# Selection matrices of a two-part graph network made three or four slots at a time

## The chip, the cores and the metric

One core of a Trainium2 chip runs the whole kernel in one launch. The metric is device time in microseconds (us) of that core. A core has five engines that run side by side and meet at semaphores: TensorE (PE, matrix products), VectorE (DVE), ScalarE (ACT), GpSimd (POOL, which here issues the gathers) and SyncE (SP, which issues transfers).

## The reference, cut to what matters

A graph with 6250 nodes of 128 features and 100,000 edges is passed through two relational layers and then two attention layers. Each layer gathers a row for each edge and sums the rows of the edges that end in the same node.

```python
def _rgcn_layer(h, src, dst, rel, basis, w_comp, loop_w, bias):
    W = jnp.einsum('rb,bio->rio', w_comp, basis)
    seg = dst * N_REL + rel
    agg = jax.ops.segment_sum(h[src], seg, num_segments=N_ENT * N_REL)
    msg = jnp.einsum('nri,rio->no', agg.reshape(N_ENT, N_REL, -1), W)
    return jax.nn.relu(msg + h @ loop_w + bias)

def _gat(x, src, dst, W, a_src, a_dst, b):
    xw = (x @ W).reshape(n, H, FH)
    e = jax.nn.leaky_relu(al_s[src] + al_d[dst], 0.2)
    ee = jnp.exp(e - jax.ops.segment_max(e, dst, num_segments=n)[dst])
    alpha = ee / jax.ops.segment_sum(ee, dst, num_segments=n)[dst]
    return jax.ops.segment_sum(alpha[:, :, None] * xw[src], dst, num_segments=n) + b
```

## The kernel before, in words

**Slots.** The edges are sorted by their end node and cut into tiles of 128 edges. A slot is one tile with one window of 128 end nodes; there are NS = 832 slots in each of the four layers. The sum of a slot is one matrix product: the gathered rows (128 edges by 128 or 136 columns, in the ring `Gr`) are multiplied by a selection matrix of 128 by 128 (in the ring `Sr`), which holds 1 where the edge's end node, `DL[:, s]` (one number in each partition), equals the column's number, `iota`. VectorE builds that matrix with one comparison, and later adds the product, which lies in a PSUM bank of `B`, to the window's sum in `AC`, a part of `XA`.

**Relational layers.** VectorE's loop runs over the slots: it makes the matrix of slot s + 8 (`selr`, a ring of SRR = 15; line 924 of the profile), waits for the product of slot s - 2 (`slot_mm`) and adds it (L935). TensorE (L1837) waits for the bank to be free (`slot_add`) or, for the first three or four slots, for `built_v`, and then for the tile to have landed, which SP relays. GpSimd's stream is one indirect gather for each tile (L2081), 782 of them in a layer, into a ring of 64 tiles; each reads 128 row numbers from `GID`.

**Attention layers.** The slots are worked on in 26 chunks of 32. While a chunk's 32 products run, the next chunk is prepared by generators that step once for a slot in its first 12 slots, and then once in two. The first eight steps of VectorE's `prep` make four matrices each (`sel`, a ring of 64; L1027). ScalarE waits for all four (`sel_made`) and casts them to bf16 in one copy of 512 columns (L1526), TensorE turns them, and softmax work follows. VectorE also weighs the gathered rows (L1103) and adds the products (L1128), and now and then weighs a finished window (L588). GpSimd gathers 830 tiles in a layer (L2098) by row numbers in `SRC`, into a ring of 96.

All orders are written out in program order on each engine; no scheduler moves anything.

Of the kernel before, what the change touches and what calls it, by code (L numbers as in the profile page):

```python
# [9 lines left out]
P = 128  # L10
# [7 lines left out]
NS = 832  # L18
# [7 lines left out]
SR = 64  # L26
TG = 64
SRR = 15
# [8 lines left out]
BIG = 1.0e30  # L37
EPS = 1e-5
LOOK, LAG = 8, 2
HS = NS // 2  # L40
HW = NW // 2
SLOW_STORES = (24, 30)
# [71 lines left out]
def build(nc, I, out, dbg=None):  # L114
# [3 lines left out]
    ALU = mybir.AluOpType  # L118
# [3 lines left out]
    with ctx:  # L122
# [14 lines left out]
        Sr = sb("Sr", [P, SR * P])  # L137
# [183 lines left out]
        def selr(s):  # L321
            return Sr[:, s % SRR * P:(s % SRR + 1) * P]

        def sel(s):
            return Sr[:, (s % SR) * P:(s % SR + 1) * P]

        def G3(c, a, b):
            o = (c * CH) % GR
# [487 lines left out]
        def vector(e):  # L816
# [85 lines left out]
            for L in range(2):  # L902
                if L == 0:
                    e.wait_ge(params, PARAMS)
                    e.wait_ge(tv.sem, tv.at("rstd"))
                    e.wait_ge(row_v, 3 * NW)
                    e.wait_ge(tg.sem, tg.at("of31"))
                    e.wait_ge(ta.sem, ta.at("oft1"))
                if L == 1:
                    for u in range(NW + NTURN - 3, NW + NTURN):  # L910
                        wait_store(e, u)
                    e.memset(x3[:, NW - 1, :], 0.0).then_inc(x0_clear, 1)
                if L == 0:
                    for u in range(NW - 3, NW):
                        wait_store(e, u)
                turn = iter(())

                def start(k):
                    return onward_vector(e, k, wregs) if L == 0 else outward_vector(e, k, wregs, xregs)
                for s in range(-LOOK, NS + LAG):  # L920
                    sn = s + LOOK
                    if sn < NS:

                        e.tensor_scalar(out=selr(sn), in0=iota[:, :], scalar1=DL[:, sn:sn + 1], scalar2=None,  # L924
                                        op0=ALU.is_equal).then_inc(built_v, 1)
                    sa = s - LAG
                    if sa >= 0:
                        if sa % 16 == 0:
                            e.reg_load(vregs[sa % 32 // 16], OFF[0:1, sa:sa + 16])
                        e.wait_ge(slot_mm, L * NS + sa + 1)  # L930
                        if vpos["self"]:
                            e.wait_ge(row_self, vpos["self"])
                            vpos["self"] = 0
                        a = AC[:, bass.ds(off(e, vregs[sa % 32 // 16][sa % 16], NW * CW), P)]
                        ins = e.tensor_tensor(a, a, B[RGCN_BANKS[L][sa % len(RGCN_BANKS[L])]][:, 0:P], ALU.add)  # L935
                        if L or sa:

                            ins._wait_ge(slot_add, L * NS + sa)
                        ins.then_inc(slot_add, 1)
                        vpos["add"] = L * NS + sa + 1  # L940
                        if L == 0 and sa % 16 == 8:
                            next(tables, None)
                        k = (sa + 1 - FIRST) // EVERY
                        if sa + 1 >= FIRST and (sa + 1 - FIRST) % EVERY == 0 and k < NK:
                            finish(turn)
                            turn = start(k)
                    next(turn, None)
                finish(turn)
                if L == 0:
                    finish(tables)  # L950
                turns = turns_of(NK, start)
                if L == 0:
                    for _ in range(2):
                        for x in turns:
                            next(x)
                    for x in turns:
                        finish(x)
                    e.wait_ge(row_self, NTURN)
                    e.wait_ge(row_a, 2 * NW + 4 * NTURN)
                    e.wait_ge(row_mm, 5 * (NW + NTURN))  # L960
                    for u in range(NW + NTURN - 3, NW + NTURN):
                        wait_store(e, u)
                    rest(e, rest_vector, "rv")
                else:
                    for _ in zip(*turns):
                        pass
                    e.wait_ge(xw_made, 2 * NTURN)
                    e.wait_ge(px, NTURN)
                    for j in range(3):
                        e.wait_ge(x1_sem[j], 16 * ((NTURN + 2 - j) // 3))  # L970
                        e.wait_ge(tg_sem[j], 16 * ((NTURN + 2 - j) // 3))
                    rest(e, rest2_vector, "r2v")
                e.nop().then_inc(rest_done, 1)
# [9 lines left out]
        def gat_vector(e, L, vregs, turns):  # L983
# [24 lines left out]
            def prep(c):  # L1008
# [8 lines left out]
                for k in range(12):  # L1017
                    if c == 0 and k < 8:

                        wait_gather(e, 2 * NG + L * NGS + 3 * k)  # L1020
                        if L and k == 0:
                            e.wait_ge(elu_parts, 26 * L)
                        av(e.memset(AC[:, k * ACP:(k + 1) * ACP], 0.0), f"AC{k}")
                    if k < 8:

                        for s in range(c0 + 4 * k, c0 + 4 * k + 4):
                            e.tensor_scalar(out=sel(s), in0=iota[:, :], scalar1=DL[:, s:s + 1], scalar2=None,  # L1027
                                            op0=ALU.is_equal).then_inc(sel_made, 1)
                    yield
                e.wait_ge(pp.sem, pp.at("ald7", t))  # L1030
                if t:
# [467 lines left out]
        def gat_scalar(e, L, wregs):  # L1499
# [4 lines left out]
            def prep(c):  # L1504
# [12 lines left out]
                for k in range(12):  # L1517
                    g = k - 1
                    if 0 <= g < 8:
                        o = ((c0 + 4 * g) % SR) * P  # L1520
                        e.wait_ge(sel_made, L * NS + c0 + 4 * g + 4)
                        if g >= 2:
                            tensor_done(f"tran{g - 2}")
                        elif t:
                            tensor_done(f"tran{g + 6}", 1)
                        then(e.copy(sbf[:, g % 2, :], Sr[:, o:o + 512]), f"cast{g}")  # L1526
                    g = k - 3
                    if 0 <= g < 8:
                        tensor_done(f"tran{g}")
                        if g >= 2:  # L1530
                            tensor_done(f"ald{g - 2}")
                        elif t:
                            tensor_done(f"ald{g + 6}", 1)
                        then(e.copy(sts[:, g % 2, :], B[3 + g % 2][:, 0:256].bitcast(bf16)), f"evac{g}")  # L1534
                    yield
# [224 lines left out]
        def tensor(e):  # L1760
# [50 lines left out]
            for L in range(2):  # L1811
# [12 lines left out]
                for s in range(-LOOK, NS + LAG):  # L1824
                    if 0 <= s < NS:
# [4 lines left out]
                        if s >= len(banks):  # L1830
                            e.wait_ge(slot_add, L * NS + s - len(banks) + 1)
                        else:
                            e.wait_ge(built_v, L * NS + s + 1)

                        e.wait_ge(landed[L], kregs[s % 32 // 16][s % 16])
                        o = off(e, pregs[s % 32 // 16][s % 16], (TG - 1) * P)
# [386 lines left out]
```

## Time and profile before

| | |
|---|---|
| time, median of 3 runs (lowest to highest) | 4555.91 us (4553.63 to 4557.06) |
| span of the profiled execution | 4547.9 us |
| GpSimd busy | 3132.4 us (69%), of it 3224 gathers |
| TensorE busy | 3121.2 us (69%) |
| VectorE busy | 2544.8 us (56%) |
| ScalarE busy | 1107.5 us (24%) |

The profiled execution has no time of its own beside its span; the median of the timed runs is 8.0 us above that span. "Busy" counts the time in which an engine executes; an engine may also be held up by the fixed work between two of its instructions, which the profile shows as idle time that ended in "issue". A gather is one instruction on GpSimd (DMA_INDIRECT), and its busy time is what GpSimd spends on issuing it, not the transfer.

### The profile page before, as it was taken

What the parts mean: (1) busy time and instruction counts of PE and PEld (TensorE: products, weight loads), DVE (VectorE), ACT (ScalarE), POOL (GpSimd) and SP (SyncE); (2) the same over time, 40 slices, a digit from 0 to 9 for tenths busy, and PEclk for the clock granted to TensorE, in tenths of its full rate; (3) what the DMA queues carried; (4) which work ended last, traced back from release to release, by engine and by line L of the source; (5) the groups of instructions that cost most, each with busy time, mean ns of one, the idle gap of its engine ahead of it and who ended that gap; (6) DMA issues with size and microseconds to landing.
All of it is one profiled execution on the core that took longest, in us unless ns stands there. A gap on an engine that the chain in (4) does not pass through costs nothing.

```text
span 4547.9 us, 63220 instructions
## 1 busy us (share of the span) xinstructions
PE 3121.2 (69%) x13439; PEld 2273.6 (50%) x13439; DVE 2544.8 (56%) x9924; ACT 1107.5 (24%) x2623; POOL 3132.4 (69%) x3271
## 2 busy tenths in 40 slices
PE   7976777777756666666646676767674666676766
PEld 3444444444434444444435555656563555565655
DVE  6534444444434455555556566767674667676776
ACT  3311222222200111111122233323332223332333
POOL 1057777777767777777677777777727777777772
PEclk9966889888855555555555566656665556665666
DMA  6633444444432222222222222222212222222222
GB/s 232 259 111 98 151 148 154 149 150 154 154 97 62 65 65 65 66 66 66 61 54 54 54 54 54 54 54 54 54 39 58 55 55 55 55 54 54 54 55 73
DMA packets 168049, 394.03 MB, mean 87 GB/s; under 512 B 57414, under 2 KB 92036, under 8 KB 150532
## 3 DMA queue, kind: packets, MB, share of 16 engines
q0 software_dynamic: 103616, 215.16, 17.9%
q10 hardware_dynamic: 37536, 102.42, 6.0%
q1 hardware_dynamic: 26532, 72.39, 4.3%
q8 instruction: 131, 2.15, 0.2%
q14 instruction: 234, 1.92, 0.1%
HBM read 229.57 MB, written 160.17 MB: 86 GB/s over the span
## 4 chain that ended last, share of the span: by engine, by line
PE 39%; DMA 15%; DVE 14%; issue 13%; POOL 11%; ACT 4%; DVEq 2%; SPq 1%; ACTq 0%; POOLq 0%
DMA Gr<-Ttab,GID 12%; PE B L1837 11%; PE B L1979 8%; POOL Gr L2098 8%; PE B L1737 6%; PE B L1799 3%; POOL Gr L2081 3%; DMA Gr<-Gtab,SRC 3%; DVE XA L1128 2%; DVE XA L935 2%; DVE Sr L1027 2%; PE B L1911 1%; PE B L1895 1%; ACT hold L1534 1%; DVE Gr L1103 1%
## 5 line engine op out<-in xcount | busy, mean ns | idle before, releaser
L2098 POOL DMA_INDIRECT Gr<-Gtab,SRC x1660 | 1603.1, 966 | 584.2 <-issue 448.5
L2081 POOL DMA_INDIRECT Gr<-Ttab,GID x1564 | 1497.3, 957 | 604.6 <-PE B L1837 272.8
L1837 PE MATMUL B<-Gr,Sr 128*128 x3328 | 999.0, 410 | 596.5 <-SPq L2114 328.6
L1837 PEld LDWEIGHTS B<-Gr,Sr 128*128 128x128 f32 x3328 | 731.3, 270 | 1051.9 <-issue 1036.4
L1979 PE MATMUL B<-Gr,Sr 128*128 128x136 f32 x3328 | 959.3, 432 | 132.9 <-DVE XA L1128 80.9
L1979 PEld LDWEIGHTS B<-Gr,Sr 128*128 128x128 f32 x3328 | 740.3, 295 | 203.7 <-DVE XA L1128 130.3
L935 DVE TENSOR_TENSOR XA<-XA,B 128x128 f32 x1664 | 471.6, 283 | 571.8 <-PE B L1837 521.3
L1128 DVE TENSOR_TENSOR XA<-XA,B 128x136 f32 x1664 | 480.8, 289 | 294.2 <-PE B L1979 237.9
L924 DVE TENSOR_SCALAR Sr<-iota,DL 128x128 f32<-128x128 f32 x1664 | 493.3, 300 | 20.6 <-issue 16.2
L1737 PE MATMUL B<-XA,H 128*128 128x512 f32 x664 | 412.5, 709 | 1.7 <-DVE H L602 0.4
L1027 DVE TENSOR_SCALAR Sr<-iota,DL 128x128 f32<-128x128 f32 x1664 | 370.2, 295 | 0.0
L1526 ACT CAST hold<-Sr 128x512 bf16<-128x512 f32 x416 | 257.2, 618 | 431.2 <-DVE Sr L1027 419.3
L1360 ACT COPY Sr<-B 128x512 f32<-128x512 f32 x332 | 194.3, 585 | 470.5 <-PE B L1737 470.5
L1895 PE MATMUL B<-identb,hold 128*128 128x128 bf16 x1664 | 232.3, 286 | 75.0 <-ACT hold L1534 48.6
L1918 PE MATMUL B<-ident,hold 128*128 128x128 f32 x52 | 23.4, 451 | 357.1 <-ACT hold L1545 357.1
L1534 ACT COPY hold<-B 128x512 bf16<-128x512 bf16 x416 | 241.7, 583 | 47.8 <-PE B L1911 45.7
L1103 DVE TENSOR_TENSOR Gr<-Gr,B 128x1024 f32<-128x1024 f32 x202 | 244.6, 1211 | 1.1 <-ACT scs L1579 1.1
L1895 PEld LDWEIGHTS B<-identb,hold 128*128 128x128 bf16 x1664 | 174.8, 132 | 117.4 <-ACT hold L1534 68.2
L1038 DVE TENSOR_TENSOR pen<-hold 128x127 f32<-128x127 f32 x52 | 15.1, 291 | 377.2 <-ACT hold L1549 377.2
L1911 PE MATMUL B<-A,hold 128*128 x1664 | 164.7, 182 | 80.5 <-ACT hold L1534 72.6
L602 DVE COPY H<-B 128x128 f32<-128x128 f32 x215 | 62.0, 289 | 270.2 <-PE B L1715 264.7
L1911 PEld LDWEIGHTS B<-A,hold 128*128 128x128 bf16 x1664 | 142.8, 113 | 123.5 <-issue 105.5
(287 smaller groups left out, 3001.2 us busy)
## 6 DMA issues: line engine op xcount, KB each, us to landing
Ttab<-Sr ACTq DMA_DIRECT2D x83, 1024.0 KB, 4.2
Ttab<-Sr SPq DMA_DIRECT2D x51, 1024.0 KB, 3.9
Gr<-Gtab,SRC POOLq DMA_INDIRECT x1660
Gr<-Ttab,GID POOLq DMA_INDIRECT x1564
Gtab<-Gr ACTq DMA_DIRECT2D x83, 66.0 KB
X1D<-Gr ACTq DMA_DIRECT2D x83, 64.0 KB
out<-Sr SPq DMA_DIRECT2D x12, 256.0 KB
Gtab<-XA SPq DMA_DIRECT2D x5, 528.0 KB, 3.8
```

Of the source, the lines that this page charges most:

```text
L924: e.tensor_scalar(out=selr(sn), in0=iota[:, :], scalar1=DL[:, sn:sn + 1], scalar2=None, op0=ALU.is_equal).then_inc(built_v, 1)
L935: ins = e.tensor_tensor(a, a, B[RGCN_BANKS[L][sa % len(RGCN_BANKS[L])]][:, 0:P], ALU.add)
L1027: e.tensor_scalar(out=sel(s), in0=iota[:, :], scalar1=DL[:, s:s + 1], scalar2=None, op0=ALU.is_equal).then_inc(sel_made, 1)
L1103: e.tensor_tensor(g, g, w, ALU.mult).then_inc(wei_v, 1)
L1128: ins = e.tensor_tensor(a, a, B[s % 3][:, 0:CW], ALU.add)
L1737: e.matmul(B[bk][:, :], hT[:, u % 2, :], wl[1][:, i * 512:(i + 1) * 512], start=True, stop=True).then_inc(row_mm, 1)
L1837: e.matmul(B[banks[s % len(banks)]][:, 0:P], selr(s), Gr[:, bass.ds(o, P)], start=True, stop=True).then_inc(slot_mm, 1)
L1895: mm = e.transpose(bt[:, j * P:(j + 1) * P], sbf[:, g % 2, j * P:(j + 1) * P], identb[:, :])
L1911: mm = e.matmul(B[5][:, 12 * m:12 * m + 12], sts[:, g % 2, j * P:(j + 1) * P], A3[:, bass.ds(off(e, regs[m % 16], 12 * NW), 12)], start=Tr ...
L1979: e.matmul(B[s % 3][:, 0:CW], sel(s), Gr[:, (s % GR) * CW:(s % GR + 1) * CW], start=True, stop=True).then_inc(gat_mm, 1)
L2081: e.indirect_dma_start(out=Gr[:, (sn + 1) % TG * P:((sn + 1) % TG + 1) * P], out_offset=None, in_=Tt[L][:, :], in_offset=bass.IndirectOffs ...
L2098: e.indirect_dma_start(out=Gr[:, (s % GR) * CW:(s % GR) * CW + 132], out_offset=None, in_=T2[L][0:NPAD][:, :], in_offset=bass.IndirectOffs ...
```

## The change

One VectorE instruction, a `tensor_tensor` comparison, makes the matrices of n neighbouring slots: its first input is `iota`, repeated n times, its second is n columns of `DL`, each repeated over 128 columns. In the relational layers n is SB3 = 3 (the last instruction of a layer makes one), and only the first two of a layer signal `built_v`; in the attention layers n is 4 with one signal. The waits on these signals are counted anew. Before, each matrix was a `tensor_scalar` comparison whose second operand was one number in each partition.

```diff
+SB3, FIRST_SETS = 3, 2
...
+        def selections(e, s, n, ring):
+            o = s % ring * P
+            return e.tensor_tensor(Sr[:, o:o + n * P].rearrange("p (s d) -> p s d", d=P),
+                                   iota[:, :].unsqueeze(1).to_broadcast([P, n, P]),
+                                   DL[:, s:s + n].unsqueeze(2).to_broadcast([P, n, P]), ALU.is_equal)
...
                     sn = s + LOOK
-                    if sn < NS:
-
-                        e.tensor_scalar(out=selr(sn), in0=iota[:, :], scalar1=DL[:, sn:sn + 1], scalar2=None,
-                                        op0=ALU.is_equal).then_inc(built_v, 1)
+                    if sn < NS and sn % SB3 == 0:
+                        ins = selections(e, sn, min(SB3, NS - sn), SRR)
+                        if sn // SB3 < FIRST_SETS:
+                            ins.then_inc(built_v, 1)
...
-                        for s in range(c0 + 4 * k, c0 + 4 * k + 4):
-                            e.tensor_scalar(out=sel(s), in0=iota[:, :], scalar1=DL[:, s:s + 1], scalar2=None,
-                                            op0=ALU.is_equal).then_inc(sel_made, 1)
+                        selections(e, c0 + 4 * k, 4, SR).then_inc(sel_made, 1)
...
-                        e.wait_ge(sel_made, L * NS + c0 + 4 * g + 4)
+                        e.wait_ge(sel_made, (L * NS + c0) // 4 + g + 1)
...
-                            e.wait_ge(built_v, L * NS + s + 1)
+                            e.wait_ge(built_v, L * FIRST_SETS + s // SB3 + 1)
```

On VectorE, in the middle of the first relational layer, the kernel before has one L924 ahead of each add (L935; L341 are the register instructions of its address).

```order
2019 L924 TENSOR_SCALAR Sr<-iota,DL 128x128
2020 L341 ISA
2021 L935 TENSOR_TENSOR XA<-XA,B 128x128
2022 L924 TENSOR_SCALAR Sr<-iota,DL 128x128
2023 L341 ISA
2024 L935 TENSOR_TENSOR XA<-XA,B 128x128
2025 L924 TENSOR_SCALAR Sr<-iota,DL 128x128
2026 L341 ISA
2027 L935 TENSOR_TENSOR XA<-XA,B 128x128
```

At the same place after the change (the add is now line 942, the helper `selections` line 330):

```order
1813 L330 TENSOR_TENSOR Sr<-iota,DL 128x384
1814 L348 ISA
1815 L942 TENSOR_TENSOR XA<-XA,B 128x128
1816 L936 TENSOR_LOAD OFF
1817 L348 ISA
1818 L942 TENSOR_TENSOR XA<-XA,B 128x128
1819 L348 ISA
1820 L942 TENSOR_TENSOR XA<-XA,B 128x128
```

Three short comparisons between the adds have become one of 384 columns ahead of the first of three adds.

On VectorE, at the start of an attention chunk, the kernel before reads as follows (L1108 loads addresses, L1119 and L1121 rescale a sum, L1128 adds):

```order
7267 L1027 TENSOR_SCALAR Sr<-iota,DL 128x128 x8
7268 L1108 TENSOR_LOAD OFF
7269 L1119 ISA
7270 L1119 TENSOR_TENSOR XA<-XA,scs 128x128
7271 L1121 ISA
7272 L1121 TENSOR_TENSOR XA<-XA,scs 128x4
7273 L341 ISA
7274 L1128 TENSOR_TENSOR XA<-XA,B 128x136
7275 L1027 TENSOR_SCALAR Sr<-iota,DL 128x128 x4
7276 L341 ISA
7277 L1128 TENSOR_TENSOR XA<-XA,B 128x136
7278 L1027 TENSOR_SCALAR Sr<-iota,DL 128x128 x4
```

And after the change, at the same place:

```order
6173 L330 TENSOR_TENSOR Sr<-iota,DL 128x512 x2
6174 L1113 TENSOR_LOAD OFF
6175 L1124 ISA
6176 L1124 TENSOR_TENSOR XA<-XA,scs 128x128
6177 L1126 ISA
6178 L1126 TENSOR_TENSOR XA<-XA,scs 128x4
6179 L348 ISA
6180 L1133 TENSOR_TENSOR XA<-XA,B 128x136
6181 L330 TENSOR_TENSOR Sr<-iota,DL 128x512
6182 L348 ISA
6183 L1133 TENSOR_TENSOR XA<-XA,B 128x136
6184 L330 TENSOR_TENSOR Sr<-iota,DL 128x512
```

Each group of four has become one instruction of 512 columns, at its old place; two of them stand back to back where eight stood.

## Rows read from the trace of the kernel before

**Rows 1.** The page's costliest groups: the selections (columns as in its heading).

```profile
L924 DVE TENSOR_SCALAR Sr<-iota,DL 128x128 f32<-128x128 f32 x1664 | 493.3, 300 | 20.6 <-issue 16.2
...
L1027 DVE TENSOR_SCALAR Sr<-iota,DL 128x128 f32<-128x128 f32 x1664 | 370.2, 295 | 0.0
```

**Rows 2.** Busy us of PE, PEld, DVE, ACT, POOL: relational layer 2, attention layer 1.

```profile
1280.80:2257.40 976.60, 646.74 (x1897) 450.23 (x1897) 482.49 (x2218) 92.54 (x325) 740.39 (x775) 0.50 0.24 66
2290.80:3330.00 1039.20, 696.65 (x3837) 587.26 (x3837) 678.31 (x2522) 316.65 (x782) 791.11 (x815) 0.60 0.21 54
```

**Rows 3.** GpSimd's gathers in each of the four layers: count, busy, mean ns.

```profile
L2081 POOL DMA_INDIRECT Gr<-Ttab,GID x782 | 750.2, 959 | 341.9 <-issue 155.5 <-DMA Ttab<-Sr 103.8 <-PE B L1837 82.6
...
L2081 POOL DMA_INDIRECT Gr<-Ttab,GID x776 | 741.3, 955 | 236.5 <-PE B L1837 190.2 <-issue 46.3
...
L2098 POOL DMA_INDIRECT Gr<-Gtab,SRC x815 | 792.1, 972 | 248.4 <-issue 190.2 <-PE B L1979 58.2
...
L2098 POOL DMA_INDIRECT Gr<-Gtab,SRC x830 | 796.5, 960 | 318.3 <-issue 254.0 <-PE B L1979 64.3
```

**Rows 4.** Timeline of GpSimd: start, duration, and in brackets the idle time before.

```profile
1273.21 0.96 POOL L2081 DMA_INDIRECT Gr<-Ttab,GID  x1 [24.66 <-DVEq L973]
...
3416.12 0.99 POOL L2098 DMA_INDIRECT Gr<-Gtab,SRC  x1 [65.69 <-issue]
...
4464.29 0.94 POOL L2098 DMA_INDIRECT Gr<-Gtab,SRC  x1 [0.30 <-issue]
```

**Rows 5.** Timeline: an add with one input in PSUM across a gather's start.

```profile
1501.24 0.29 DVE L935 TENSOR_TENSOR XA<-XA,B 128x128 f32 x1 [0.51 <-PE B L1837]
1501.34 0.95 POOL L2081 DMA_INDIRECT Gr<-Ttab,GID  x1 [0.30 <-PE B L1837]
```

**Rows 6.** Timeline: selections and gathers at the start of two attention chunks.

```profile
2371.57 0.86 DVE L1027 TENSOR_SCALAR Sr<-iota,DL 128x128 f32<-128x128 f32 x4
...
2371.99 1.07 POOL L2098 DMA_INDIRECT Gr<-Gtab,SRC  x1 [0.30 <-issue]
...
2372.35 0.28 DVE L1119 TENSOR_TENSOR XA<-XA,scs 128x128 f32 x1
...
2374.07 0.86 DVE L1027 TENSOR_SCALAR Sr<-iota,DL 128x128 f32<-128x128 f32 x4
...
2374.68 1.08 POOL L2098 DMA_INDIRECT Gr<-Gtab,SRC  x1 [0.31 <-issue]
...
2412.87 1.07 POOL L2098 DMA_INDIRECT Gr<-Gtab,SRC  x1 [0.30 <-PE B L1979]
...
2415.57 1.08 POOL L2098 DMA_INDIRECT Gr<-Gtab,SRC  x1 [0.30 <-issue]
```

**Rows 7.** Timeline: VectorE instructions with both inputs in SBUF across a gather's start.

```profile
2704.75 0.86 DVE L1027 TENSOR_SCALAR Sr<-iota,DL 128x128 f32<-128x128 f32 x4
...
2705.37 1.41 POOL L2098 DMA_INDIRECT Gr<-Gtab,SRC  x1 [0.30 <-PE B L1979]
...
2705.54 0.42 DVE L588 TENSOR_TENSOR H<-XA,GID 128x256 f32 x1
...
4195.41 0.55 DVE L1167 TENSOR_TENSOR GID<-GID,wt 128x392 f32<-128x392 f32 x1
4195.48 1.29 POOL L2098 DMA_INDIRECT Gr<-Gtab,SRC  x1 [0.30 <-issue]
...
4278.43 0.42 DVE L588 TENSOR_TENSOR H<-XA,GID 128x256 f32 x1 [0.67 <-ACT XA L1599]
4278.48 1.19 POOL L2098 DMA_INDIRECT Gr<-Gtab,SRC  x1 [0.30 <-PE B L1979]
```

**Rows 8.** VectorE's groups by shape between 2500 and 3100 us.

```profile
L1103 DVE TENSOR_TENSOR Gr<-Gr,B 128x1024 f32<-128x1024 f32 x58 | 70.3, 1211 | 0.0
L588 DVE TENSOR_TENSOR H<-XA,GID 128x256 f32 x40 | 16.7, 418 | 7.4 <-DVE XA L1213 6.3 <-ACT XA L1599 1.0
...
L1187 DVE TENSOR_TENSOR GID<-GID,st 128x392 f32<-128x392 f32 x3 | 1.7, 553 | 0.0
```

## Prediction

> **What bounds the kernel now.** I read the busy shares first. They name nobody: GpSimd and TensorE both stand at 69%, VectorE at 56%. So I went by stage. In the second relational layer VectorE is busy 482 of 977 us and in the first attention layer 678 of 1039 [rows 2]; in neither is it full, and GpSimd's "busy" is about 76% in both. What GpSimd's missing quarter is, its own groups and timeline tell. In the second relational layer 776 gathers take 741.3 us and the idle time before them is 236.5 us, which is 0.305 us for each; in the first attention layer 248.4 us over 815 is 0.305 us again [rows 3]. The timeline shows the same 0.30 or 0.31 us ahead of each gather, whoever is named as releaser. A wait that never gets longer or shorter is no wait but the fixed step between two gathers. So GpSimd runs one gather in 0.95 + 0.30 = 1.26 us, without a gap, through each layer. Its only real holes are the ones between layers, of which two are shown, 24.66 us and 65.69 us [rows 4]. The last gather begins at 4464.29 us [rows 4], and what follows is the tail of 84 us. From about 260 us to that point the time is 3224 gathers times their step: **GpSimd sets the end, VectorE does not**. A VectorE instruction is worth something here only in what it does to a gather.
>
> **What a gather suffers from VectorE.** Mean durations differ by layer: 959 and 955 ns in the relational layers, 972 and 960 in the attention layers [rows 3], though the instruction is the same and a quiet one takes 0.94 or 0.95 [rows 4, 5]. So I looked at the long ones and at what VectorE did as they began.
> - At 4278.48 a gather begins while L588, a `tensor_tensor` with both inputs in SBUF, is running. L588 ends at 4278.85, which is 0.37 us behind the gather's start; the gather takes 1.19, 0.24 more than a quiet one [rows 7].
> - At 4195.48 it is L1167, also with both inputs in SBUF, until 0.48 behind the start: 1.29, or 0.34 more [rows 7].
> - At 2705.37 a burst of selections runs until 0.24 behind the start and L588 follows at once until 0.59: 1.41, or 0.46 more [rows 7]. So a second such instruction can carry the hold on.
> - At 1501.34 an add whose second input is in PSUM runs until 0.19 behind the start: 0.95, nothing [rows 5].
>
> The pattern is: extension = end of the VectorE instruction behind the gather's start, less 0.13 us, if it was running when the gather began and reads two SBUF tensors. The gather stands still until VectorE is through. L588 is the best stand-in for the new instruction, as it too has an input that is repeated along columns by a broadcast.
>
> The selections of today do it as well, but they are short. In an attention chunk two gathers start inside a burst of four (2371.99 and 2374.68) and take 1.07 and 1.08; the burst at 2371.57 goes on until 0.44 behind the start, yet costs only 0.12, so the gather slips in after one of its parts [rows 6]. The next chunk has the same two [rows 6].
>
> The Trainium skill (SBUF — State Buffer, § Who interferes with whom) says that a Vector instruction with two SBUF inputs contends with a GpSimd instruction that reads SBUF and that the second one to issue blocks fully; by that rule the trace agrees. The same section also says that `tensor_tensor`, as it holds only the read side, does not stall descriptor generation, marked there as inferred, while `tensor_scalar` in its two-port form does; by that rule the change would take the holds away.
>
> **The change part by part.**
> 1. *Removed on VectorE.* 1664 L924 at 300 ns and 1664 L1027 at 295 ns [rows 1]. In a burst, four take 0.86 us, as they overlap [rows 6].
> 2. *Added on VectorE.* 554 instructions of 384 columns (the last of each layer has 128) and 416 of 512. The trace has none of these; the nearest are 256 columns at 418 ns, 392 at 553, 1024 at 1211 [rows 8]. From 392 to 1024 the slope is 658 / 632 = 1.04 ns a column, so 384 takes 553 - 8 = 545 ns and 512 takes 553 + 125 = 678 ns. Four selections thus fall from 0.86 to 0.68 us, three from about 0.8 to 0.55. VectorE gains some 100 to 250 us of busy time in all. On the path this is worth nothing: VectorE idles half of a relational layer and a third of an attention layer [rows 2]. If gathers were free, it would be worth looking at; they are not.
> 3. *Signals.* The signals dropped had no one waiting (TensorE waits on the add of a slot three back). The cast waited for the fourth matrix anyway. Cost and gain nothing, hidden behind the gathers; without that cover, some 0.1 us a chunk step.
> 4. *Holds given back.* From [rows 6], 2 x 0.12 us a chunk over 52 chunks is 12.5 us; the relational means are 2 to 6 ns above 953, of which I give the selections 3 us in all. Together **-15 us**. The upper bound is everything above a quiet gather: (972 - 953) x 815 + (960 - 944) x 830 + (959 - 953) x 782 + (955 - 953) x 776 = 35 us; the lower is nothing.
> 5. *Holds added.* Let a new instruction of length D fall anywhere in the gather's step of 1.26 us. It does harm if it was running at the start and ends later than 0.13 behind it: a share (D - 0.13) / 1.26, with a mean harm of (D - 0.13) / 2.
>    - D = 0.545: 0.33 x 0.21 = 0.068 us, times 554 = **+38 us** in the relational layers.
>    - D = 0.678: 0.43 x 0.27 = 0.119 us, times 416 = **+50 us** in the attention layers. A look at the order agrees: eight of them within 8 adds, some 0.68 of every 0.9 us, while six gathers start, gives 6 x 0.6 x 0.27 = 0.97 us a chunk, 51 us in 52.
>    - The first two of a chunk stand back to back, as one hold of 1.3 us if the gather can't slip in between. That is (1.27 - 0.13) / 1.26 x 0.57 = 0.52 us where two alone give 0.24; over 50 chunks 14 us more at most, none at least. I take half, **+7 us**.
>
> The ends for 5: none, if broadcast inputs hold nothing (a rival below). At the upper end the relational part doubles: there VectorE's step follows the landing of a tile, so the place of the instruction in the gather's step is not drawn afresh each time, and it can sit where it does harm; 76 + 64 = 140 us. It can also sit in a harmless place half of the time: 19 + 35 = 54 us.
>
> What is late next when a gather is held: all later gathers of the layer, as the stream has no gap to make it good; then the landing, TensorE's product and the add, all by the same amount. The layers' seams and the tail have no selections on their path, so they stay.
>
> **The sum**, against the profiled execution: 4547.9 - 15 + 38 + 50 + 7 = 4627.9 us. The median of the runs stands 8.0 us above that span, so **4636 us**, 1.8% more than 4555.9.
>
> **The rivals.**
> - *No hold, a gain.* If the two-tensor comparison doesn't hold gathers, because one input is `iota` repeated and the other a few numbers, item 5 goes and item 4 stays: 4556 - 15 = 4541 us, at best 4521. Against it: L588 has a broadcast input and holds. It decides where a new instruction costs under 15 us / 970 = 15 ns on average against my 98. Chance 0.06.
> - *No change.* Holds in harmless places only, or compensated by item 4: 4556 us, within 9 us. Chance 0.04.
> - *Locked in a bad place.* In the relational layers the instruction sits across a gather's start every time: 0.2 to 0.39 us x 554 = 110 to 216 us there; with 42 net from the rest, 4708 to 4814. For it: VectorE does follow landings. Against: in [rows 5] the add sits across the start and today's next ones elsewhere, turns and windows push VectorE about. Chance 0.1.
> - *Forecast*, holds spread over the step: 4585 to 4700. Chance 0.8.
>
> **How the numbers follow.** What a measurement of this kernel can tell from no change is about 0.2%, 9 us. Slower by more: 0.8 + 0.1 = 0.90; same 0.04; faster 0.06. The forecast's ends are 4556 - 15 + 54 = 4595, taken down to 4585 as the price of 0.13 is a reading of three gathers, and 4556 - 15 + 140 = 4681, plus 19 for holds that other instructions carry on, 4700.
>
> **What would show it.** In the profile of the changed kernel: gathers still 0.30 us apart; their mean up by some 20 ns in the relational layers and by 30 or so in the attention layers; line 330 at 545 and 678 ns; single gathers of 1.2 to 1.5 us with line 330 running at their start and ending 0.13 us before the extension does; VectorE's busy time down. It is wrong if long gathers don't coincide with line 330, if the means fall, or if gaps over 0.31 us appear in the stream, as then something else has become the bound.

## The result and the profile after

The changed kernel takes 4606.26 us (median of 4 runs, 4606.23 to 4608.01), beside 4554.77 us for the kernel before on the same chip: a ratio of 1.0114, interval 1.0101 to 1.0126. It is slower by 51.5 us. The profiled execution has a span of 4606.2 us.

The page's costliest groups of the changed kernel, gathers first (L2103 attention, L2086 relational), then the adds and the new comparison L330:

```profile
L2103 POOL DMA_INDIRECT Gr<-Gtab,SRC x1660 | 1633.8, 984 | 583.6 <-issue 449.8
L2086 POOL DMA_INDIRECT Gr<-Ttab,GID x1564 | 1516.7, 970 | 611.7 <-PE B L1842 260.0
...
L942 DVE TENSOR_TENSOR XA<-XA,B 128x128 f32 x1664 | 475.1, 286 | 658.5 <-PE B L1842 584.4
L1133 DVE TENSOR_TENSOR XA<-XA,B 128x136 f32 x1664 | 484.6, 291 | 338.0 <-PE B L1984 277.1
L330 DVE TENSOR_TENSOR Sr<-iota,DL 128x384 f32<-128x384 f32 (+1 forms) x972 | 592.3, 610 | 4.0 <-DMA Ttab<-Sr 3.8
```

VectorE now makes all selections in 592.3 us, where the two groups of [rows 1] took 863.5. Nothing came of it: its idle time ahead of the adds grew instead (L942, L1133). The gathers' own busy time grew by 30.7 us in the attention layers and 19.4 us in the relational ones, while the idle time before them is as it was. By layer, the four stretches that answer to [rows 3]:

```profile
L2086 POOL DMA_INDIRECT Gr<-Ttab,GID x782 | 764.9, 978 | 341.8 <-issue 159.7 <-DMA Ttab<-Sr 103.8 <-PE B L1842 78.3
...
L2086 POOL DMA_INDIRECT Gr<-Ttab,GID x782 | 751.8, 961 | 269.9 <-PE B L1842 181.7 <-issue 56.4 <-DVEq L980 31.8
...
L2103 POOL DMA_INDIRECT Gr<-Gtab,SRC x830 | 821.2, 989 | 266.0 <-issue 195.1 <-PE B L1984 57.6 <-DVEq L980 13.3
...
L2103 POOL DMA_INDIRECT Gr<-Gtab,SRC x830 | 812.6, 979 | 317.6 <-issue 254.8 <-PE B L1984 62.8
```

The means rose from 959, 955, 972 and 960 ns to 978, 961, 989 and 979. Times the count of 782 or 830 this is +15, +5, +14 and +16 us: 50 us, the whole of the slowdown. In all four layers no gap between two gathers is over 0.32 us.

The timeline of the changed kernel shows how, one place each in the two relational layers and the first attention layer:

```profile
565.00 0.55 DVE L330 TENSOR_TENSOR Sr<-iota,DL 128x384 f32<-128x384 f32 x1
565.03 1.34 POOL L2086 DMA_INDIRECT Gr<-Ttab,GID  x1 [0.30 <-issue]
...
1704.43 0.96 POOL L2086 DMA_INDIRECT Gr<-Ttab,GID  x1 [0.31 <-PE B L1842]
1704.59 0.55 DVE L330 TENSOR_TENSOR Sr<-iota,DL 128x384 f32<-128x384 f32 x1
...
2401.64 0.69 DVE L330 TENSOR_TENSOR Sr<-iota,DL 128x512 f32<-128x512 f32 x1
2401.80 1.35 POOL L2103 DMA_INDIRECT Gr<-Gtab,SRC  x1 [0.30 <-issue]
2402.25 0.29 DVE L1133 TENSOR_TENSOR XA<-XA,B 128x136 f32 x1
...
2402.45 0.69 DVE L330 TENSOR_TENSOR Sr<-iota,DL 128x512 f32<-128x512 f32 x1
```

At 565.03 a gather begins 0.03 us into an L330; the comparison ends 0.52 behind the gather's start, and the gather takes 1.34 us, which is 0.39 more. At 2401.80 the comparison ends 0.53 behind the start, and the gather takes 1.35. At 1704.43 the comparison starts 0.16 behind the gather's start, and the gather takes its usual 0.96 although the two run side by side. The hold is there only if the comparison was running first. At 2402.25 an add stands between this chunk's first two comparisons.

Counted over the whole trace, 339 gathers start under an L330, and 281 of them with more than 0.18 us of it to come. 244 of these are extended by the end of the comparison less 0.11 to 0.145 us (the median is 0.127). Another 36 are not extended at all; in each the comparison had begun at most 0.035 us before the gather (only two gathers as near to the comparison's start were held). There it is the comparison that is late, by some 0.04 to 0.08 us, as here (0.74 us for 0.69):

```profile
4104.84 0.74 DVE L330 TENSOR_TENSOR Sr<-iota,DL 128x512 f32<-128x512 f32 x1
4104.85 0.94 POOL L2103 DMA_INDIRECT Gr<-Gtab,SRC  x1 [0.30 <-issue]
```

If each gather's time above its layer's median is put down to what VectorE ran at its start, L330 took 16.7, 5.0, 21.8 and 22.8 us in the four layers, 66 in all. The selections of the kernel before, counted the same way, took 2.0, 0.5, 8.5 and 5.9, 17 in all. The difference of 49 us is the slowdown.

The stretches of [rows 2], and the first gathers behind two seams with the last gather of all, which answer to [rows 4]:

```profile
1296.30:2286.00 989.70, 647.68 (x1899) 450.40 (x1899) 455.38 (x1677) 92.56 (x325) 751.60 (x782) 0.50 0.24 67
2299.50:3373.00 1073.50, 689.68 (x3861) 580.70 (x3861) 651.70 (x1932) 321.08 (x788) 820.86 (x830) 0.60 0.22 53
```

```profile
1296.30 0.96 POOL L2086 DMA_INDIRECT Gr<-Ttab,GID  x1 [31.75 <-DVEq L980]
...
3457.74 0.99 POOL L2103 DMA_INDIRECT Gr<-Gtab,SRC  x1 [64.94 <-issue]
...
4522.06 0.95 POOL L2103 DMA_INDIRECT Gr<-Gtab,SRC  x1 [0.31 <-issue]
```

VectorE went from 482 to 455 us in the second relational layer and from 678 to 652 in the first attention layer. The seam between the attention layers (64.94 us) and the tail (84.1 us) stayed. The first seam grew from 24.66 to 31.75 us in this execution. The other profiled executions below with three banks in that layer had 25 to 29 us there, in no order that follows the edits, so I do not count these 7 us as the change's. With the 50 us of the gathers they make the 58 us by which the two spans differ. The medians differ by 51; that the seam is shorter in the other executions is not shown.

### The profile page after: what moved, and what is told of

Read it like the earlier page. It is cut to its first block, busy times and chain, and to the rows that moved or that the text cites. A ratio compares the mean times of both kernels' runs of the same rounds, so it can differ in the third digit from the quotient of the medians.

```text
span 4606.2 us, 60864 instructions
## 1 busy us (share of the span) xinstructions
PE 3115.0 (68%) x13439; PEld 2263.0 (49%) x13439; DVE 2423.1 (53%) x7568; ACT 1109.4 (24%) x2623; POOL 3182.5 (69%) x3271
## 4 chain that ended last, share of the span: by engine, by line
PE 40%; DMA 15%; issue 13%; DVE 13%; POOL 11%; ACT 4%; DVEq 2%; SPq 1%; ACTq 0%; POOLq 0%
DMA Gr<-Ttab,GID 12%; PE B L1842 10%; PE B L1984 9%; POOL Gr L2103 8%; PE B L1742 7%; POOL Gr L2086 4%; PE B L1804 3%; DMA Gr<-Gtab,SRC 3%; DVE XA L1133 2%; DVE XA L942 2%; PE B L1916 2%; DVE Sr L330 2%; PE B L1900 2%; ACT hold L1539 1%; PE B L599 1%
## 5 line engine op out<-in xcount | busy, mean ns | idle before, releaser
L2103 POOL DMA_INDIRECT Gr<-Gtab,SRC x1660 | 1633.8, 984 | 583.6 <-issue 449.8
L2086 POOL DMA_INDIRECT Gr<-Ttab,GID x1564 | 1516.7, 970 | 611.7 <-PE B L1842 260.0
L1984 PE MATMUL B<-Gr,Sr 128*128 128x136 f32 x3328 | 947.1, 427 | 131.4 <-DVE XA L1133 75.5
L942 DVE TENSOR_TENSOR XA<-XA,B 128x128 f32 x1664 | 475.1, 286 | 658.5 <-PE B L1842 584.4
L1133 DVE TENSOR_TENSOR XA<-XA,B 128x136 f32 x1664 | 484.6, 291 | 338.0 <-PE B L1984 277.1
L330 DVE TENSOR_TENSOR Sr<-iota,DL 128x384 f32<-128x384 f32 (+1 forms) x972 | 592.3, 610 | 4.0 <-DMA Ttab<-Sr 3.8
L1742 PE MATMUL B<-XA,H 128*128 128x512 f32 x664 | 429.1, 735 | 1.7 <-DVE H L609 0.4
L1108 DVE TENSOR_TENSOR Gr<-Gr,B 128x1024 f32<-128x1024 f32 x202 | 245.1, 1213 | 1.2 <-ACT scs L1584 1.1
L1923 PEld LDWEIGHTS B<-ident,hold 128*128 128x128 f32 x52 | 9.3, 179 | 424.0 <-ACT hold L1550 424.0
```

Source lines behind the costliest of these rows:

```text
L330: return e.tensor_tensor(Sr[:, o:o + n * P].rearrange("p (s d) -> p s d", d=P), iota[:, :].unsqueeze(1).to_broadcast([P, n, P]), DL[:, s:s ...
L1133: ins = e.tensor_tensor(a, a, B[s % 3][:, 0:CW], ALU.add)
L1742: e.matmul(B[bk][:, :], hT[:, u % 2, :], wl[1][:, i * 512:(i + 1) * 512], start=True, stop=True).then_inc(row_mm, 1)
L1984: e.matmul(B[s % 3][:, 0:CW], sel(s), Gr[:, (s % GR) * CW:(s % GR + 1) * CW], start=True, stop=True).then_inc(gat_mm, 1)
L2086: e.indirect_dma_start(out=Gr[:, (sn + 1) % TG * P:((sn + 1) % TG + 1) * P], out_offset=None, in_=Tt[L][:, :], in_offset=bass.IndirectOffs ...
L2103: e.indirect_dma_start(out=Gr[:, (s % GR) * CW:(s % GR) * CW + 132], out_offset=None, in_=T2[L][0:NPAD][:, :], in_offset=bass.IndirectOffs ...
```

## Experiments

Ratios are to the kernel before on the chip of the same call. A quiet gather is not equally long everywhere: the median of the second relational layer was 955 ns in some profiles and 958 in others. Gathers are therefore compared by the long ones, over 1.1 us, where the mean alone would mislead. The kernel before has 3, 0, 10 and 22 of them in its four layers (782, 782, 830 and 830 gathers), the changed one 58, 16, 77 and 71. In layers that an edit left alone this count can vary too: 34 and 27 in the attention layers of the first kernel below, for 10 and 22.

### One half of the change at a time

```diff
 # relational alone: the attention layers as before
-                        selections(e, c0 + 4 * k, 4, SR).then_inc(sel_made, 1)
+                        for s in range(c0 + 4 * k, c0 + 4 * k + 4):
+                            e.tensor_scalar(out=sel(s), in0=iota[:, :], scalar1=DL[:, s:s + 1], ...)
 # attention alone: the relational layers as before
-                    if sn < NS and sn % SB3 == 0:
-                        ins = selections(e, sn, min(SB3, NS - sn), SRR)
+                    if sn < NS:
+                        e.tensor_scalar(out=selr(sn), in0=iota[:, :], scalar1=DL[:, sn:sn + 1], ...)
```

> The change in the relational layers alone (sets of three there, single comparisons in the attention layers). Theory of held gathers (a VectorE instruction with two SBUF inputs that runs at a gather's start holds the gather until 0.13 us before its end): the gathers of the changed kernel grew by 15 us in the first relational layer and by 4 in the second, so the time is 4555 + 19 = 4574 us, 4581 if the first seam's 7 us belong to it, and the attention gathers keep their means of 970 and 958 ns. Rival, the slower chain (the comparison of 545 ns delays the adds behind it and so frees the ring late): then the idle time between gathers would be over 0.31 us in places, and the gathers' own durations as before. Rival, all of the loss comes from the attention layers: 4555 us.

Measured: 4587.8 us, ratio 1.0046 (1.0030 to 1.0063); on this chip the kernel before took 4564.66. By the ratio that is +21 us, by the medians +23, for +19 expected. 58 and 19 long gathers in the relational layers, no gap over 0.32 us. The attention layers were expected at 970 and 958 ns and had 978 and 964.

> The change in the attention layers alone (four to an instruction there, single comparisons in the relational layers). Theory of held gathers: the attention gathers grew by 14.4 and 16.1 us, so 4555 + 30 = 4585 us, relational gathers at 957 and 953 ns and the first seam at 24.7 us again. Rival, the slower chain: gaps over 0.31 us between gathers and durations as before. Rival, the loss is all relational: 4555 us.

Measured: 4595.94 us, ratio 1.0067 (1.0050 to 1.0083), +31 us for +30 expected. 96 and 85 long gathers in the attention layers, 3 and 0 in the relational ones, whose means are 962 and 958 ns for 957 and 953 expected. The halves add up (0.46% and 0.67%, together 1.13%), as extensions of one serial stream must. The two kernels ran on one chip, and each is the other's control: the relational gathers take 21 us more in the first, the attention gathers 33 us more in the second. Where a half is as before, its means are up by 3 to 6 ns all the same, most of it in the quiet gather: the last attention layer of the first kernel, then the second relational layer of the second:

```profile
L2105 POOL DMA_INDIRECT Gr<-Gtab,SRC x830 | 799.8, 964 | 318.4 <-issue 258.0 <-PE B L1986 60.4
```

```profile
L2086 POOL DMA_INDIRECT Gr<-Ttab,GID x782 | 749.4, 958 | 264.7 <-PE B L1842 184.2 <-issue 54.0 <-DVEq L980 26.5
```

### Taking the second SBUF input away

The comparison reads `iota` from PSUM. No bank was free, so the slot products gave one up, and a control kernel gives it up and changes nothing else.

```diff
-RGCN_BANKS = ((0, 1, 2), (0, 1, 2, 7))
+RGCN_BANKS = ((0, 1), (0, 1, 7))
...
+        iotap = B[2][:, 384:512]
...
-                                   iota[:, :].unsqueeze(1).to_broadcast([P, n, P]),
+                                   iotap.unsqueeze(1).to_broadcast([P, n, P]),
...
-                    e.matmul(B[s % 3][:, 0:CW], sel(s), Gr[...], start=True, stop=True)
+                    e.matmul(B[s % 2][:, 0:CW], sel(s), Gr[...], start=True, stop=True)
```

> The whole change, but the comparisons read the column numbers (iota) from PSUM, bank 2, so each has one input in SBUF only. To free that bank the slot products use two banks in place of three (three in place of four in the second relational layer), in all layers. Theory of held gathers: no comparison holds a gather; what is left are the other instructions with two SBUF inputs (some 10 us), and the comparisons' old share of some 15 us is gone too: gather means 954 to 963 ns, no gather over 1.1 us with a comparison at its start; 4555 - 15 = 4540 us, give or take 8, with the comparisons as long as in the changed kernel (545 and 678 ns). Rival, length alone (any long VectorE instruction disturbs a gather): 4606 us as with the change. Rival, fewer banks make TensorE late: gaps between gathers over 0.31 us, also in the next kernel, which has only the fewer banks.

> The kernel before with two banks for the slot products in place of three (three in place of four in the second relational layer); nothing else. All theories: TensorE and VectorE keep slack behind the gathers, so 4555 us within 9. If the banks cost something, it shows here by itself, and is to be taken off the run with the numbers in PSUM.

Measured: 4689.42 us (1.0272, 1.0255 to 1.0289) with `iota` in PSUM, and 4721.39 us (1.0343, 1.0326 to 1.0361) for the control. My expectation of both times was wrong, as the bank has a price of 3.4%. The control shows where. The gathers' waits between 600 and 1320 us, in its first relational layer (engine, line, who was waited for, us in total, times, longest), and the first gather behind that layer:

```profile
POOL Gr L2081 <- issue: 120.9, 372, 1.7
POOL Gr L2081 <- PE B L1837: 97.1, 149, 2.5
```

```profile
1416.71 0.97 POOL L2081 DMA_INDIRECT Gr<-Ttab,GID  x1 [100.46 <-DVEq L973]
```

There TensorE has the turned rows' products to do beside the slots, and with two banks it falls behind the gathers. In that layer it waits 210 us (261 times) for the add that frees the bank, where the kernel before has 113 us (125 times). The gathers have 113 gaps over 0.33 us, 65 us more than the usual step in all, and a backlog makes the seam 100 us where it was 25. The seam between the attention layers and the tail grew by 8 to 10 us each. Inside the second relational layer and the attention layers there is no gap at all.

The question on the input is answered within the gathers. In the kernel with `iota` in PSUM (the comparison is L333 there, as long as before):

```profile
366.21 0.55 DVE L333 TENSOR_TENSOR Sr<-B,DL 128x384 f32<-128x384 f32 x1
366.45 0.96 POOL L2093 DMA_INDIRECT Gr<-Ttab,GID  x1 [0.30 <-issue]
...
433.64 0.55 DVE L333 TENSOR_TENSOR Sr<-B,DL 128x384 f32<-128x384 f32 x1
...
433.81 0.96 POOL L2093 DMA_INDIRECT Gr<-Ttab,GID  x1 [0.30 <-issue]
...
2545.87 0.68 DVE L333 TENSOR_TENSOR Sr<-B,DL 128x512 f32<-128x512 f32 x1
2545.90 0.95 POOL L2110 DMA_INDIRECT Gr<-Gtab,SRC  x1 [0.30 <-issue]
```

Each of the first two comparisons was running when the gather began and went on 0.31 and 0.38 us behind its start; the gather took 0.96 us. The third, of four slots, goes on 0.65 us behind the start, and the gather takes 0.95. In the whole trace 175 gathers start 0.04 us or more into such a comparison with over 0.3 us of it to come; all 175 take 0.94 to 0.96 us. In the changed kernel there are 172 such gathers, and none takes under 1.12 us. The means of the relational layers are back at 959 and 957 ns, with 3 and 0 long gathers. The attention layers keep 42 and 26 long ones, 37 and 28 in the control; none of those 42 and 26 starts under a comparison. Length alone is out; the second SBUF input is what holds. The time shows it as well, against the control: 32 us less, 25 in the spans, of which 14 lie in the first relational layer and the seam behind it and 11 in the attention layers.

### Length and form

```diff
 # one slot to an instruction, attention layers (relational: SB3 = 1)
-                        selections(e, c0 + 4 * k, 4, SR).then_inc(sel_made, 1)
+                        for s in range(c0 + 4 * k, c0 + 4 * k + 4):
+                            ins = selections(e, s, 1, SR)
+                        ins.then_inc(sel_made, 1)
 # longer (relational: SB3 = 5)
-                        selections(e, c0 + 4 * k, 4, SR).then_inc(sel_made, 1)
+                    if k < 8 and k % 2 == 0:
+                        selections(e, c0 + 4 * k, 8, SR).then_inc(sel_made, 1)
```

> The changed form (tensor_tensor with iota and a broadcast column of DL) but one slot to an instruction: 128 columns, some 283 ns, as many instructions as in the kernel before. Tells form from length. Theory of held gathers, where length decides: the same as the single comparisons before, within 9 us of the kernel before on this chip (ratio 0.998 to 1.002), few gathers over 1.1 us in the relational layers. Rival, the form decides (two tensor inputs hold a gather and a per-partition scalar hardly does): ratio 1.007 to 1.012, as with the change.

Measured: 4610.93 us, ratio 1.0125 (1.0109 to 1.0140). By the ratio the rival won, by place both were half right. In the relational layers, where an add stands between two comparisons, there are 3 and 0 long gathers, as before the change: a hold there is as short as the instruction. Nearly all of the loss is in the attention layers, whose gathers take 29 and 25 us more. Its gathers in the first relational and the first attention layer:

```profile
L2088 POOL DMA_INDIRECT Gr<-Ttab,GID x782 | 753.9, 964 | 341.8 <-issue 144.7 <-DMA Ttab<-Sr 103.8 <-PE B L1844 93.2
...
L2105 POOL DMA_INDIRECT Gr<-Gtab,SRC x830 | 835.1, 1006 | 266.0 <-issue 191.3 <-PE B L1986 61.2 <-DVEq L980 13.4
```

The comparisons come in bursts of four. 68 gathers of the two attention layers take over 1.5 us, like the second one here:

```profile
2383.36 0.89 DVE L330 TENSOR_TENSOR Sr<-iota,DL 128x128 f32<-128x128 f32 x4
2383.46 1.02 POOL L2105 DMA_INDIRECT Gr<-Gtab,SRC  x1 [0.30 <-issue]
...
2389.57 1.72 POOL L2105 DMA_INDIRECT Gr<-Gtab,SRC  x1 [0.31 <-PE B L1986]
2389.57 0.89 DVE L330 TENSOR_TENSOR Sr<-iota,DL 128x128 f32<-128x128 f32 x4
```

At 2389.57 the burst starts with the gather, all four run until 0.89 behind its start, and the gather takes 1.72 us, 0.76 more. At 2383.46 the gather starts 0.10 into a burst and slips in after the first part. So a burst of `tensor_tensor` comparisons can hold like one long instruction, and need not: of 187 gathers that start in one with over 0.5 us of it to come, 65 wait for its end, 69 lose at most 0.13 us and 48 nothing. What decides between them is open. In the kernel before there are 159 such gathers, in bursts of `tensor_scalar`, and none waits for the end.

> The changed form with longer instructions: five slots (640 columns, some 811 ns) in the relational layers, eight (1024 columns, some 1211 ns) at every second step in the attention layers. The harm of one grows with the square of (length less 0.13 us), the number falls: by the formula of the prediction, scaled by what the change gave of it (half in the relational layers, 0.8 in the attention layers), +31 and +62 us, so ratio 1.020, from 1.014 to 1.026; single gathers of up to 2.0 us. Rival, a fixed price for each instruction (issue, signals): fewer instructions, so a ratio under the change's 1.011.

Measured: 4666.03 us, ratio 1.0245 (1.0229 to 1.0260), inside the expected 1.014 to 1.026. Fewer instructions cost more, so there is no fixed price for each. The instructions' lengths, and the gathers of the first relational layer:

```profile
L330 DVE TENSOR_TENSOR Sr<-iota,DL 128x640 f32<-128x640 f32 x49 | 40.1, 818 | 0.0
...
L330 DVE TENSOR_TENSOR Sr<-iota,DL 128x1024 f32<-128x1024 f32 x76 | 92.6, 1219 | 0.1
```

```profile
L2086 POOL DMA_INDIRECT Gr<-Ttab,GID x782 | 785.2, 1004 | 341.9 <-issue 151.5 <-DMA Ttab<-Sr 103.8 <-PE B L1842 86.6
```

The relational layers took 35 and 16 us more than the kernel before, the attention layers 30 and 34; at the change's length these were 15, 5, 15 and 16. The split was expected as 31 and 62 and is 51 and 64, so nearly the whole miss is in the relational layers. The 62 was too low for its own working: 208 instructions of 1.211 us by the formula, times 0.8, give 77. Against that, the step from four to eight slots cost less than the formula says.

### Which instruction lets a gather in

```diff
+                        for s in range(c0 + 4 * k, c0 + 4 * k + 4):
+                            if s % 2:
+                                ins = e.tensor_scalar(out=sel(s), in0=iota[:, :], ...)
+                            else:
+                                selections(e, s, 1, SR)
+                        ins.then_inc(sel_made, 1)
```

> Relational layers as in the kernel before; in the attention layers four selections of one slot each, in turn tensor_tensor and tensor_scalar. The kernel with tensor_tensor alone held a gather through a whole burst (up to 0.78 us), the kernel before with tensor_scalar alone through one or two parts. Theory that only tensor_tensor behind tensor_tensor carries a hold on, and that a gather slips in behind a tensor_scalar: no gather held over 0.45 us at a selection, attention layers some 10 us longer than before together, ratio 1.000 to 1.005. Rival, any burst with tensor_tensor in it holds to its end: ratio 1.009 to 1.013, gathers of 1.7 us.

Measured: 4558.12 us, ratio 1.0007 (0.9998 to 1.0016), so no different from the kernel before. Its longest gathers in the attention layers are one each of 1.42, 1.38 and 1.30 us. The first of them lies in a burst of comparisons and waits for its end, 0.46 us, just over the 0.45 that I had allowed; of 167 gathers that start in such a burst with over 0.5 us to come, it is the only one. A gather inside such a burst (L1035 is the `tensor_scalar`, L330 the `tensor_tensor`):

```profile
2375.92 0.28 DVE L1035 TENSOR_SCALAR Sr<-iota,DL 128x128 f32<-128x128 f32 x1
2376.12 0.29 DVE L330 TENSOR_TENSOR Sr<-iota,DL 128x128 f32<-128x128 f32 x1
2376.13 1.10 POOL L2109 DMA_INDIRECT Gr<-Gtab,SRC  x1 [0.30 <-issue]
...
2376.32 0.28 DVE L1035 TENSOR_SCALAR Sr<-iota,DL 128x128 f32<-128x128 f32 x1
```

It began 0.01 us into a `tensor_tensor` that ends 0.28 behind its start, and takes 1.10 us, 0.15 more; the `tensor_scalar` that follows to 0.47 does not carry the hold on. With `tensor_tensor` alone a burst held a gather by up to 0.76 us.

### A version that is faster than both

`iota` in PSUM where a bank can be spared: three banks in the second relational layer, two in the attention layers with the third one back for a layer's last chunk, when no selection is made any more. The first relational layer is as in the kernel before. One kernel has the grouped comparisons, the other single `tensor_scalar` ones.

```diff
+        def bank_of(s):
+            return B[s % 2 if s < NS - CH else (s - NS + CH) % 3]
```

> The change where a PSUM bank can be spared: in the second relational layer (three banks for products in place of four) and in the attention layers (two in place of three, three again in the last chunk of a layer) the grouped comparison reads iota from PSUM bank 2; the first relational layer keeps the single comparisons of the kernel before. Theory of held gathers: second relational layer 1 to 2 us faster than before, each attention layer 5 to 8 us faster, seams and tail as before thanks to the third bank in the last chunk: ratio 0.997, from 0.995 to 0.999. Rival, two banks cost the attention seams their 9 us each in any case: ratio 1.001 to 1.002.

> The same banks and the same iota in PSUM, but single tensor_scalar comparisons throughout, as in the kernel before. Tells whether grouping itself is worth anything once no comparison holds a gather. Theory that GpSimd's stream sets the time: the same as the grouped form with iota in PSUM, within 5 us, though VectorE is busy some 120 to 200 us longer. Rival, VectorE's time is worth something behind the gathers' cover, at seams and tail: 10 us or more slower than the grouped form.

Measured: 4544.59 us (0.9979, 0.9970 to 0.9989) grouped and 4543.31 us (0.9979, 0.9970 to 0.9988) single. Both are faster than the kernel before by 8 to 10 us, and with that than the changed one too. The busy line of the page, grouped, then single:

```profile
PE 3232.5 (71%) x13439; PEld 2304.1 (51%) x13439; DVE 2442.2 (54%) x8123; ACT 1111.2 (24%) x2623; POOL 3123.0 (69%) x3271
```

```profile
PE 3254.6 (72%) x13439; PEld 2321.2 (51%) x13439; DVE 2683.1 (59%) x9925; ACT 1113.0 (24%) x2623; POOL 3120.1 (69%) x3271
```

VectorE is busy 241 us longer with single comparisons and the time is the same. (I had expected 120 to 200; a single comparison takes 340 ns with `iota` in PSUM, for 297 with it in SBUF.) Grouping by itself is worth nothing here. No seam and no tail grew by more than 5 us.

> The version with iota in PSUM where a bank is free, and one more instruction taken off the shared inputs: the first scan of a chunk's preparation reads its second input from PSUM (where TensorE left it) and no longer ScalarE's copy in SBUF. Theory of held gathers: the scan held some 45 gathers by 0.14 to 0.19 us, 7 us in all, so the ratio falls from 0.998 to 0.9965 (0.9950 to 0.9975), and the gathers that start under a scan take 0.95 us. Rival, the next instruction of the chain holds the same gather instead, or the gathers' stream meets other holders at its new places: ratio 0.998 as before.

```diff
-                then(e.tensor_tensor_scan(FB[:, 0, :], pen[:, 0:P], xt, -BIG, ALU.add, ALU.max), "s1")
+                then(e.tensor_tensor_scan(FB[:, 0, :], pen[:, 0:P], B[6][:, P:2 * P], -BIG, ALU.add, ALU.max), "s1")
```

Measured: 4539.67 us, ratio 0.9965 (0.9952 to 0.9979), the lowest ratio of all. The interval overlaps that of the version without this edit, so a gain is not shown by the times. The trace shows both theory and rival: the 38 gathers under the scan lost 5.5 us in the version without the edit, and its 41 here lose nothing, but 25 gathers under a later scan (L1073, both inputs in SBUF) lose 3.0 us where 24 lost 0.2. The long gathers of the attention layers fell from 30 and 19 to 23 and 15, which is less than such counts vary between profiles of the same layers.

## Why the prediction was right, point by point

- *GpSimd sets the end*: shown. The stream has no gap in any of the kernels but those with two banks in the first relational layer, and the gathers' busy time accounts for 50 of 51.5 us. VectorE's 122 us less of busy time in the changed kernel bought nothing, nor did the 241 us between the grouped and the single version.
- *The hold ends with the instruction, less 0.13 us*: shown (0.127 in the median of 245 extended gathers), and its cause by the comparison that reads `iota` from PSUM. The sum took it that only a comparison that runs first holds a gather; so it is (1704.43). What it did not have is that a comparison which began at most 0.035 us before the gather hardly ever holds it: 36 of the 281 gathers lose nothing.
- *Prices of the comparisons*: 545 and 678 ns were forecast; 0.55 us and 0.68 to 0.69 us are on the timeline.
- *Relational layers, +38 less 3*: measured 20, of it 22 added and 2.5 given back. The even spread over the gather's step held in the first layer: it lets 0.545 / 1.26 = 43% of 277 sets lie across a gather's start, which is 120, and there are 123, with 17 us for 19. In the second it did not: 33, with 5 us for 19, and so the mean rose by 6 ns there and not by some 20. There 199 of 278 L330 start in the first half microsecond of the step, as at 1704.59, where they harm nobody. That its place is set by the landing of the tiles is argued from the timeline; no run shifted it.
- *Attention layers, +50 + 7 less 12*: measured 30 and confirmed by the half alone (31); 45 were added and 14 given back. The net is off by a third. The 7 us for the two back to back had no object. The order shown ahead of the prediction holds once in each attention layer, near its start; everywhere else an add stands between the two, as at 2402.25 above, so that there are 2 such pairs in the kernel and not 50. For the other 50 us the even spread was too much by 5: the chunk's instructions come at nearly the same place of the gather's step in many chunks (the last of the eight starts about 0.6 us behind a gather's start in 29 of 52, where it harms nobody), and on the whole these places were kinder than the average.
- *The sum, 4636, and its range*: 30 us too high, as all these errors lean one way. The measured time lies near the lower end of the range, which allowed for harmless places; so the mechanism was right, and the size was covered by the width of the range. The lower end's 35 us for the attention layers has no working (half of 50 + 7 would be 28).
- *Seams and tail stay*: so they did, within what they vary.
- *The rivals*: a gain from a comparison that holds nothing is excluded for this input, and came true, with 8 to 10 us, once `iota` lay in PSUM where a bank was free. The bad lock did not occur. The Trainium skill (SBUF — State Buffer, § Who interferes with whom) has both rules that I weighed: two SBUF inputs contend with a GpSimd instruction that reads SBUF, and this case agrees (1.34 us for 0.95); `tensor_tensor` does not stall descriptor generation, marked there as inferred, and here the measurement decides against it for an indirect gather, by 50 us in 4555.

## What to carry to other kernels

Find the engine whose stream has the same step between any two of its instructions; then ask of a change on another engine not how much time it saves there but what it does to that step. Where GpSimd issues gathers back to back, a VectorE instruction with two SBUF inputs costs up to its own length, less 0.13 us here, for each gather that starts under it, and several in a row can count as one: keep them short and apart, or read one input from PSUM. Before giving up a PSUM bank for that, try the bank alone: here it cost 3.4% in all, most of it in one layer and the seam behind it (142 of the 170 us between the two profiled spans), 18 us at the last seam and the tail. The other 10 us are no more than a quiet gather's variation between profiles makes.

## What the runs showed of the hardware that I had not expected

- Four `tensor_tensor` of 128 columns in a row can hold a gather for the whole burst (1.72 us; 65 of 187), while alternating with `tensor_scalar` it gets in earlier (1.10 us; one of 167 waits for the end). A single comparison of either form hardly holds: there is no gather over 1.1 us in the second relational layer with 832 of the one (the kernel before) or of the other (one slot to an instruction).
- The border between the two orders is sharp: a comparison with over 0.18 us to come held the gather in every case in which it had begun over 0.035 us before it. Where it had begun nearer, the gather took its usual time, in 36 of 38 cases, and the comparison was longer by 0.04 to 0.08 us.
- A quiet gather is 955 ns in one profile and 958 in another of the same instructions (medians of the second relational layer in the kernel before and in that with the change in the attention layers alone); times 3224 this is 10 us, as much as some effects looked for here. It is not the chip alone: the kernel with alternating forms (955) and the last one above, with the scan's input in PSUM (958), ran on one chip.
